# Round two of a graph attention and state-space kernel: one accumulator pair, the D term on TensorE, a scan for the polynomial

## The reference

```python
# layer 1: graph attention on LN(x)
e   = leaky_relu(x @ a[:F] + (x @ a[F:]).T, 0.2)
U   = softmax(where(adj > 0, e, -9e15), axis=1)
prop_u = U @ x;  rowsum = sum(U * 0.5 * U, axis=1)
feat   = soft_threshold(mix of x, prop_u, x * rowsum)
pu     = U @ feat
out    = mix of feat, pu, h0 with coefficients sigmoid(temp)
# layer 2: one Mamba-2 block on LN(x + out), chunks of 128 rows
z, xBC, dt = split(x @ W_in)
xBC = silu(causal conv of 4 taps);  dt = softplus(dt + dt_bias)
Y   = Y_diag + Y_off + xh * D
Y   = Y * silu(z);  Y = Y * rsqrt(mean(Y*Y) + eps) * norm_w
out = (Y @ W_out) @ W_lin + b_lin
```

## Time and profile before

| | |
|---|---|
| three timed runs | 965.16, 971.51, 972.10 us |
| the profiled execution | 977.07 us, span 975.1 us, mean granted TensorE clock 0.935 |
| PE busy | 871.6 us (89%), 6586 matmuls |
| PE weight loads busy | 776.6 us (80%) |
| DVE busy | 771.0 us (79%), 2057 instructions |
| POOL busy | 645.5 us (66%), 1359 instructions |
| ACT busy | 595.4 us (61%), 1032 instructions |
| chain that ended last | POOL 44%, PE 21%, issue 15%, DVE 10%, DMA 5%, ACT 5% |

### The profile page before, as it was taken

One profiled execution on the slowest core, in us unless ns is written; L12 is line 12 of the kernel. 1 busy time (PEld: TensorE's weight loads), 2 busy tenths in 40 slices (PEclk: granted clock), 3 DMA queues, 4 the chain that ended last, 5 costly groups with the idle time before them and its releaser, 6 DMA issues.

```text
span 975.1 us, 21990 instructions
## 1 busy us (share of the span) xinstructions
PE 871.6 (89%) x6586; PEld 776.6 (80%) x6586; DVE 771.0 (79%) x2057; ACT 595.4 (61%) x1032; POOL 645.5 (66%) x1359
## 2 busy tenths in 40 slices
PE   5858999989989999559899898999899989999976
PEld 5648999989989999549788787878778877888844
DVE  6477999979979996576989778777787778688873
ACT  3556788868778885336566556555556656565541
POOL 3550665656665667886768787877776877777743
PEclk9969999999989999859999999999989999899975
DMA  7356887968778686001111111111111111110000
GB/s 212 101 179 216 259 267 215 315 219 267 261 217 279 190 271 203 1 23 61 55 36 56 44 47 47 42 36 48 37 56 32 51 38 51 35 33 17 4 7 9
DMA packets 97386, 110.66 MB, mean 113 GB/s; under 512 B 6433, under 2 KB 89121, under 8 KB 97313
## 3 DMA queue, kind: packets, MB, share of 16 engines
q1 hardware_dynamic: 97312, 109.68, 35.6%
HBM read 90.79 MB, written 18.87 MB: 112 GB/s over the span
## 4 chain that ended last, share of the span: by engine, by line
POOL 44%; PE 21%; issue 15%; DVE 10%; DMA 5%; ACT 5%; POOLq 1%; DVEq 0%; ACTq 0%; SPq 0%
PE accA L1239 6%; POOL featw L510 5%; PE accC L1248 5%; DMA adj_in<-in_adj_dram 4%; POOL f_rows L547 3%; POOL adj_in L545 3%; PE ps L1186 3%; ACT edges L989 3%; POOL adj_in L549 2%; POOL featw L508 2%; POOL ywork L551 2%; POOL f_rows L558 2%; DVE code L642 2%; POOL adj_in L514 1%; POOL featw L513 1%
## 5 line engine op out<-in xcount | busy, mean ns | idle before, releaser
L1239 PE MATMUL accA<-Y,maskA 128*128 128x260 f32 (+1 forms) x2048 | 321.3, 301 | 28.6 <-DVE Y L621 18.1
L1239 PEld LDWEIGHTS accA<-Y,maskA 128*128 128x128 f32 x2048 | 273.7, 198 | 48.5 <-issue 24.6
L1025 ACT ACTIVATE maskA<-code 128x1024 fp32r<-128x1024 int8 x256 | 268.6, 1051 | 58.2 <-PE accC L1248 30.1
L1248 PE MATMUL accC<-Y,maskC 128*128 128x260 f32 (+1 forms) x2048 | 299.3, 290 | 1.4 <-DVE maskC L650 1.4
L1248 PEld LDWEIGHTS accC<-Y,maskC 128*128 128x128 f32 x2048 | 272.6, 196 | 1.9 <-DVE maskC L650 1.8
L650 DVE TENSOR_SCALAR maskC<-code 128x1024 fp32r<-128x1024 int8 x256 | 209.1, 821 | 0.3 <-issue 0.3
L642 DVE SCALAR_TENSOR_TENSOR code<-f_rows,neg_f,ps 128x512 int8<-128x512 f32 x256 | 178.4, 740 | 29.2 <-PE ps L1186 27.8
L989 ACT ACTIVATE edges<-adj_in 128x1024 bf16<-128x1024 f32 x128 | 133.3, 1045 | 27.5 <-DMA adj_in<-in_adj_dram 14.9
L1186 PE MATMUL ps<-ident,edges 128*128 128x128 bf16 x1024 | 82.7, 225 | 16.3 <-DVE code L642 10.8
L870 DVE SCALAR_TENSOR_TENSOR code<-adj_in,f_rows,code 128x128 f32<-128x128 f32 x288 | 94.9, 351 | 0.0
L1186 PEld LDWEIGHTS ps<-ident,edges 128*128 128x128 bf16 x1024 | 60.7, 101 | 27.1 <-issue 12.3
(11 more groups left out here) (199 smaller groups left out, 1588.5 us busy)
## 6 DMA issues: line engine op xcount, KB each, us to landing
adj_in<-in_adj_dram SPq DMA_DIRECT2D x128, 512.0 KB, 4.5
edge_codes<-code SPq DMA_DIRECT2D x8, 2048.0 KB, 10.0
code<-edge_codes SPq DMA_DIRECT2D x32, 512.0 KB, 3.3
xn<-in_x_dram SPq DMA_DIRECT2D x4, 512.0 KB, 5.6
adj_in<-in_x_dram SPq DMA_DIRECT2D x32, 64.0 KB, 1.8
adj_in<-in_L_gnn_h_dram SPq DMA_DIRECT2D x32, 64.0 KB, 1.9
out_dram<-adj_in SPq DMA_DIRECT2D x32, 64.0 KB, 1.6
f_rows<-in_L_ffn_W_in_dram SPq DMA_DIRECT2D x1, 192.0 KB, 6.5
```

The costliest lines, as they stand in the source:

```text
L1025: s.activation(maskA[:, b % MASKS], src, ACT.Relu, bias=-2.0).then_inc(S["maskA_ready"], 1)
L1239: t_.matmul(accA[k][:, 0:2 * cols], maskA[:, b % MASKS, l * P:(l + 1) * P], Y[:, jt, 0, :, 0:cols], start=jt == 0, stop=jt == NT - 1)
L1248: m = t_.matmul(accC[k][:, 0:2 * cols], maskC[:, b % MASKS, l * P:(l + 1) * P], Y[:, jt, 1, :, 0:cols], start=jt == 0, stop=jt == NT - 1)
```

## The change

- **Accumulators.** Round two uses accA0 and accC0 for all row tiles. PE's first product of a slot waits until ACT has read accA (`acc_read`) and DVE has read accC (a new semaphore `c_read`) for the row tile before. ACT's read waits for a new semaphore `a_done`, raised by the last A product, which comes before the last C block; before it waited for both.
- **Banks.** accA1 takes the new state (columns 0 to 255) and the transpose of xn2 (256 to 383); accC1 takes the output product. Before they were in ps1 and ps0. The output product now waits for `out_done`, the state product no longer.
- **C without the turn.** DVE writes C straight from the conv into `cT` (partitions 0 to 63 of a zeroed 128-row tile, two buffers); the product with the identity (L1380) and ACT's copy (L1159) are gone, and the products with C run over 128 rows.
- **D term.** `xD` on POOL (L549) and its addition on DVE (L905) are gone; PE adds the conv output times diag(D) into the chunk product's bank, two products of 128 by 128 by 128 a slot. diag(D) is made once on DVE.
- **Polynomial.** Seven small DVE steps (the square, a scale, four Horner steps, the last product) become one square written five times, one `tensor_tensor_scan` over 24 elements, and one product.
- **Base scalars.** Six POOL operations over all 32 row tiles, once, take the place of a copy and six small operations in each slot.
- **Order.** DVE's output row moves from the head of the slot to behind the gated output. POOL's x1b moves from behind the inverse root to behind the decayed state.
- **Start.** `row_shift` leaves DVE; ACT does it with two Relu activations, and DVE makes two biases. ACT's first two high parts move in between its f1 copies.

```diff
+    def over_rows(i, j):
+        return coef[:, i:j].broadcast_to([P, NT])
+    r_all, zn_all, rho_all, kap_all = (row_out[:, :, i] for i in range(4))
+    link(g.tensor_tensor(kap_all, rho_all, over_rows(1, 2), ALU.mult))
+    link(g.tensor_tensor(kap_all, kap_all, over_rows(8, 9), ALU.add))
+    link(g.tensor_tensor(rho_all, kap_all, over_rows(10, 11), ALU.mult))
+    link(g.tensor_tensor(rho_all, rho_all, over_rows(1, 2), ALU.add))
+    link(g.tensor_tensor(r_all, r_all, rho_all, ALU.mult))
+    link(g.tensor_tensor(zn_all, r_all, zn_all, ALU.mult))
+    end_chain()
...
+    g.memset(state[:], 0.0)
+    g.memset(cT, 0.0)
+    g.memset(horner[:, 0], 0.0)
+    for i in range(6):
+        g.memset(horner[:, 1, :, i], log_c[5 - i])
     g.memset(hist[:, 0, :, 0:TAPS - 1], 0.0).then_inc(S["halo_done"], 1)
...
         wait(pool, f"rowx_in{k % 2}", (s_ - k % 2) * 16 + 32)
-        link(g.tensor_copy(small[:, 8:12], row_out[:, bass.ds(row, 1), :].rearrange("p a b -> p (a b)")))
-        r, zn, rho = (small[:, i:i + 1] for i in (8, 9, 10))
-        link(g.tensor_tensor(kap, coef[:, 1:2], rho, ALU.mult))
-        link(g.tensor_tensor(kap, kap, coef[:, 8:9], ALU.add))
-        link(g.tensor_tensor(wz, kap, coef[:, 10:11], ALU.mult))
-        link(g.tensor_tensor(wz, wz, coef[:, 1:2], ALU.add))
-        wait(pool, "x1_done", s_ - 1)
-        link(g.tensor_tensor(w, wz, r, ALU.mult))
-        link(g.tensor_tensor(wz, w, zn, ALU.mult))
-        link(g.tensor_tensor(featw[:, 0], xn[:, bass.ds(row, 1), :].rearrange("p a b -> p (a b)"),
-                             kap.broadcast_to([P, F]), ALU.mult))
+        step_to(g.tensor_tensor(featw[:, 0], xn[:, bass.ds(row, 1), :].rearrange("p a b -> p (a b)"), kap.broadcast_to([P, F]), ALU.mult))
         link(g.tensor_tensor(featw[:, 1], h0_in[:, k % 2], coef[:, 9:10].broadcast_to([P, F]), ALU.mult))
         link(g.tensor_tensor(featw[:, 0], featw[:, 0], featw[:, 1], ALU.add))
         link(g.tensor_tensor(featw[:, 0], featw[:, 0], x_in[:, k % 2], ALU.add))
+        wait(pool, "x1_done", s_ - 1)
...
-            wait(pool, "y_read", s_ - 3)
-            g.tensor_tensor(heads(xD, HD), heads(xl[:, 0:DI], HD), d_row.unsqueeze(2).broadcast_to([P, NH, HD]), ALU.mult).then_inc(S["xD_ready"], 1)
...
+        if ok[0]:
+            kt = (k - 1) % SLOTS
+            wait(pool, "x1_done", s_)
+            wait(pool, "out_done", s_ - 4)
+            g.tensor_tensor(x1b[:, kt], x1[:, kt % 2], b_row, ALU.add).then_inc(S["x1b_done"], 1)
...
-    def row_shift():
-        step(v.tensor_scalar(hcol[:, 0], fcol[:, :, 0], grow[:, 6:7], 1.0 - SLOPE, ALU.add, ALU.mult))
-        link(v.tensor_scalar(hcol[:, 1], fcol[:, :, 0], grow[:, 6:7], SLOPE - 1.0, ALU.add, ALU.mult))
-        v.tensor_scalar(hcol[:, 0], hcol[:, 0], 0.0, -SHIFT, ALU.min, ALU.add)
-        v.tensor_scalar(hcol[:, 1], hcol[:, 1], 0.0, None, ALU.min).then_inc(S["roww_done"], 1)
...
     v.tensor_scalar(conv_bt, conv_bt, 0.5, None, ALU.mult).then_inc(S["w_ready"], 1)
+    dve.wait_ge(S["signed"], NG * BLOCKS)
+    for kb in range(KB):
...
-            halves = step(v.scalar_tensor_tensor(
-                out=part, in0=accC[kt][:, 0:2 * F].rearrange("p (a b) -> p a b", a=2),
-                scalar=roww[:, bass.ds(row, 1), 1:2].rearrange("p a b -> p (a b)"), in1=acc_s[:, kt, :, 0:F], op0=ALU.mult, op1=ALU.add))
+            dve.wait_ge(S["mm_done"], T * NB + (R1 + NB))
+            v.scalar_tensor_tensor(
+                out=part, in0=accC[0][:, 0:2 * F].rearrange("p (a b) -> p a b", a=2),
+                scalar=roww[:, bass.ds(row, 1), 1:2].rearrange("p a b -> p (a b)"), in1=acc_s[:, kt, :, 0:F],
+                op0=ALU.mult, op1=ALU.add).then_inc(S["c_read"], 1)
...
-        if ok[4]:
-            dve.wait_ge(S["rs_ready"], s_ - 4)
-            wait(dve, f"stored{1 - k2}", (s_ - 5 - (1 - k2)) * 8)
-            v.scalar_tensor_tensor(out=outb[:, 1 - k2], in0=ps[1][:, P:P + F], scalar=tiny[:, 6, 2:3], in1=x1b[:, (k - 1) % SLOTS],
-                                   op0=ALU.mult, op1=ALU.add).then_inc(S["out_done"], 1)
         if ok[0]:
-            dve.wait_ge(S["vch"], halves)
+            dve.wait_ge(S["c_read"], T + 1)
             halves = step(v.tensor_tensor(part[:, 0], part[:, 0], part[:, 1], ALU.add))
...
-                dve.wait_ge(S["xD_ready"], s_ - 3)
                 dve.wait_ge(S["ps_ready"], s_ - 3)
                 summed_y[0] = step(v.tensor_tensor(heads(ysum), heads(ps[0][:, DI:2 * DI]),
                                                    tiny[:, 4 + k2, 0:NH].unsqueeze(2).broadcast_to([P, NH, HD]), ALU.mult))
-                v.tensor_tensor(state[0:DS, 1 - k2], pstate[0:DS], ps[1][0:DS, 0:DI], ALU.add).then_inc(S["st_done"], 1)
-        def y_skip():
-            if ok[3]:
-                dve.wait_ge(S["vch"], summed_y[0])
-                summed_y[0] = step(v.tensor_tensor(ysum, ysum, xD, ALU.add))
+                v.tensor_tensor(state[0:DS, 1 - k2], pstate[0:DS], accA[1][0:DS, 0:DI], ALU.add).then_inc(S["st_done"], 1)
...
-            last = step(v.tensor_tensor(z, si, si, ALU.mult))
+            last = step(v.tensor_tensor(horner[:, 0, :, 1:6], si.unsqueeze(2).broadcast_to([P, NH, 5]),
+                                        si.unsqueeze(2).broadcast_to([P, NH, 5]), ALU.mult))
             conv_step(7)
             dve.wait_ge(S["vch"], last)
-            last = step(v.tensor_scalar(p, z, log_c[-1], None, ALU.mult))
+            last = step(v.tensor_tensor_scan(horner[:, 2].rearrange("p h c -> p (h c)"), horner[:, 0].rearrange("p h c -> p (h c)"),
+                                             horner[:, 1].rearrange("p h c -> p (h c)"), 0.0, ALU.mult, ALU.add))
             conv_step(8)
-            others = [None, None, normalise2, y_state, y_skip]
-            for cf, other in zip(log_c[-2:0:-1] + [None], others):
-                dve.wait_ge(S["vch"], last)
-                if cf is None:
-                    last = step(v.scalar_tensor_tensor(out=p, in0=p, scalar=log_c[0], in1=si, op0=ALU.add, op1=ALU.mult))
-                else:
-                    last = step(v.scalar_tensor_tensor(out=p, in0=p, scalar=cf, in1=z, op0=ALU.add, op1=ALU.mult))
-                if other is not None:
-                    other()
+            dve.wait_ge(S["vch"], last)
+            last = step(v.tensor_tensor(p, horner[:, 2, :, 5], si, ALU.mult))
+            normalise2()
+            y_state()
...
             dve.wait_ge(S["y_read"], s_ - 3)
             wait(dve, "p_yT", s_ - 4)
             wait(dve, "ssq_ready", s_ - 4)
             v.tensor_tensor(yg, ysum, gate[:, k2], ALU.mult).then_inc(S["yg_ready"], 1)
+        if ok[4]:
+            dve.wait_ge(S["p_o"], s_ - 4)
+            dve.wait_ge(S["rs_ready"], s_ - 4)
+            wait(dve, f"stored{1 - k2}", (s_ - 5 - (1 - k2)) * 8)
+            v.scalar_tensor_tensor(out=outb[:, 1 - k2], in0=accC[1][:, 0:F], scalar=tiny[:, 6, 2:3], in1=x1b[:, (k - 1) % SLOTS],
...
-            v.scalar_tensor_tensor(out=xbc[:, k2], in0=gate_t, scalar=1.0, in1=conv, op0=ALU.add, op1=ALU.mult).then_inc(S["conv_ready"], 1)
+            wait(dve, "p_y", s_ - 3)
+            v.scalar_tensor_tensor(out=xbc[:, k2], in0=gate_t, scalar=1.0, in1=conv, op0=ALU.add, op1=ALU.mult)
+            v.scalar_tensor_tensor(out=cT[0:DS, k2], in0=gate_t[DS:P, CB - 1], scalar=1.0, in1=conv[DS:P, CB - 1], op0=ALU.add,
+                                   op1=ALU.mult).then_inc(S["conv_ready"], 1)
...
-        act.wait_ge(S["mm_done"], T * NB + (NB + round_two * R1))
         if round_two:
+            act.wait_ge(S["a_done"], T + 1)
             wait(act, "x1_done", T - 1)
         else:
+            act.wait_ge(S["mm_done"], T * NB + NB)
             wait(act, "scaled_done", T - 1)
         w = roww[:, bass.ds(row, 1), 0:1].rearrange("p a b -> p (a b)")
-        src = accA[k][:, 0:2 * cols].rearrange("p (a b) -> p a b", a=2)
+        src = accA[0 if round_two else k][:, 0:2 * cols].rearrange("p (a b) -> p a b", a=2)
         s.mul(acc_s[:, k, :, 0:cols], src, w).then_inc(S["acc_read"], 1)
...
+            y_high_one(q, 0)
             sign(0, 4)
             f1_copy(3)
+            y_high_one(q, 1)
             f1_copy(4)
             sign(0, 5)
             for c in range(5, 8):
                 f1_copy(c)
-        y_high(q)
+        else:
+            y_high_one(q, 0)
+            y_high_one(q, 1)
+        if q == 0:
+            s.activation(hcol[:, 0], fcol[:, :, 0], ACT.Relu, bias=grow[:, 8:9], scale=SLOPE - 1.0)
+            s.activation(hcol[:, 1], fcol[:, :, 0], ACT.Relu, bias=grow[:, 9:10], scale=1.0 - SLOPE).then_inc(S["roww_done"], 1)
...
+            m = t_.matmul(accA[k][:, 0:2 * cols], maskA[:, b % MASKS, l * P:(l + 1) * P], Y[:, jt, 0, :, 0:cols],
+                          start=jt == 0, stop=jt == NT - 1)
+        if cols == F and ch == NB - 1:
+            m.then_inc(S["a_done"], 1)
...
-                    wait(pe, "x1_done", s_ - 1)
+                    if isinstance(s_, int) and s_ == 0:
```

(38 more changed lines are left out.)

96 lines of the change are left out of this document (46 added, 50 removed).

## The result

The changed kernel takes 997.95 us (median of four, 996.08 to 999.41); the kernel before took 968.92 in the same comparison (four, 965.16 to 972.10). The ratio is 1.030, 95% interval 1.025 to 1.034: slower by 3%. Forecast were 949 us and a range of 929 to 967, and slower by over 1% had a chance of 0.09. The profiled execution took 998.5 us, with a span of 996.8. One execution of a kernel further down, e1_two_pairs, fell in a slow state (1143.8 us, granted clock 0.66) and is left out of its ratio.

The account below looks back on a forecast made before the run. Round two was taken as bound by a POOL-DVE ring. Loop -16, unrolled slots +1.5, diag(D) +0.6, start -5.5 and tail -3 sum to -22.4 us: profiled 977.1 becomes 954.7, median 971.5 becomes 949; range 929 to 967.

Parts of the forecast that it names:

- The new wait: Round two: PE starts block 0 only when both accumulators are read, ACT's read being late; 0.85 us every slot.
- DVE's ring: Round two: chain from DVE's accC read through block 0 and DVE's stream to the next read; 15.6 us a slot.
- The scan's price: DVE's polynomial in round two: the scan taken as 0.17 us, between 0.15 and 0.41.
- The collision rival: Round two: DVE and POOL stretch one another's instructions, slot 16.3 us, 965 us in all; chance 0.24.
- PE's own time: Round two: PE's work without stalls, 14.67 - 0.43 + 0.55 = 14.8 us a slot.
- The clock rival: Round two: the pause at block 0 lowers PE's clock every slot, losing 2 us; slot 17.7, 1001 us; chance 0.09.
- The hidden drain: Round two: ACT reads accA in time, PE alone bounds at 14.8 us a slot; 926 us; chance 0.12.
- First slots: Round two's first slots, 440 to 478 us: some waits won, the drain paid instead; 0.
- POOL's leaving the path: Round two: POOL's chain falls from 13.2 to 11.0 us a slot and no longer bounds it.
- the start: Kernel start: row_shift leaves DVE, whose codes come earlier; -5.5 us, bounds 0 and -7.
- the row's move: Round two: DVE's output row no longer ahead of x1, so POOL's late end no longer starts the next slot; unsized.
- POOL's ring: Round two before the change: POOL's 13.2 us chain plus DVE's 2.3 make the slot, 16.50 us in the loop.

Follow-up runs that it names:

- e1_two_pairs: The changed kernel with two accumulator pairs in round two again, small products' new banks undone too; 898.8 us, ratio 0.924 to the kernel before.
- h1a: The changed kernel with one added wait: POOL's base products start only after DVE's last conv step; 945.7 us, ratio 0.980 to the kernel before.
- g12: e1_two_pairs with DVE's output row back at the slot's head and the base scalars again made slot by slot on POOL; 928.5 us, ratio 0.952.
- h1b: e1_two_pairs with POOL's base products waiting for DVE's last conv step; 892.8 us, ratio 0.926 to the kernel before.
- g6: e1_two_pairs with the zero-padded products taken over 64 rows or 64 columns of weights again; 923.5 us, ratio 0.945 to the kernel before.
- e2: The changed kernel, still one accumulator pair, with DVE reading accC ahead of C's small product and the fourth mask; 937.2 us, ratio 0.965.
- e5: The changed kernel with ten unused transposes on PE at the end of each slot from 4 to 31; 981.3 us, ratio 1.009.
- e4: The kernel before with only the single accumulator pair edits, small products' banks unchanged; 987.8 us, ratio 1.017 to the kernel before.
- g1: e1_two_pairs with DVE's output row back at the slot's head, behind the first mask; 901.2 us, ratio 0.924 to the kernel before.
- g3: e1_two_pairs with the polynomial in seven small DVE steps again; 921.5 us, ratio 0.945 to the kernel before.

## Why the prediction was wrong

**The step that failed is "The new wait", with DVE's ring behind it.** The forecast put the wait at 0.85 us and on ACT, which would be busy up to its read of accA. ACT had read 2.1 us early; DVE held PE for 2.50 us. The forecast had the ring that does this, and sized it at 15.6 us; at the high clock it measures 16.38. By its own pieces: to `in_read` 5.16 (forecast 5.3); L864 to the end of the output row 6.12 (5.4); from there to gm, with C's product, 4.29 (4.05); gm and the read 0.80 (0.8). So 0.7 of the missing 0.8 us is in the stretch that holds the polynomial. The scan's price, 0.17 as a step, was well chosen for a scan alone: it lasts 0.20 in h1a and g12. What was left out is that the base scalars, once removed from POOL, bring POOL's 128-wide products under these very steps, which stretches four of them by 0.93 us in all: the first of these products starts 1.5 us behind L864, where it was 4.0 behind L860 before. There it stood beside two small steps nearer the end (L949 and L952, 0.38 and 0.30 us on the mean), so a part of the stretching is not new. h1a shows the cause, for with the products later that stretch of DVE's stream takes 5.24 us and not 6.12. The collision rival had this mechanism on the masks alone, and gave 16.3 us a slot, the ring's true size. The Trainium skill (SBUF — State Buffer, "Who interferes with whom") says that a DVE instruction with two SBUF inputs contends with a GpSimd instruction that reads SBUF; the trace agrees, 0.43 against 0.17 us for the square.

**PE's own time** was 1.2 too high: 14.8 forecast, 13.61 with nothing in its way (h1b; 13.76 in e1_two_pairs). The padding, costed at nothing, is 0.73 of that by g6 against e1, or 0.88 against h1b. The D products cost 0.45 us by the timeline (0.55 forecast). Between a PE time that was too long and a ring through DVE that was too short the forecast saw two level rings; in truth they are 2.6 us or more apart, and PE pauses for the difference. The ring isn't DVE's load: DVE does the same work in 13.76 us with two pairs (e1). It is a chain through PE, ACT and DVE that only the single pair closes.

**The clock rival** happened in half of the slots. The forecast had it decide from a slot of 16.9 us with 2.5 us at 1.2 GHz in each; measured are 1.37 us in every second one, 0.69 on the mean, so that 16.38 becomes 17.07. Its place was right and its chance, 0.09, too low, for it was hung on a pause of 0.85 that was never measured. That its 1001 us lies beside the measured 998 is luck: it had 2 us of low clock in each slot and the ring at 15.7, where the ring is longer, the clock's share smaller, and the first slots lose 19 us that it had at nothing. Pauses of 1.27 (e2), 1.40 (h1a) and 1.43 us (e5) left the clock up in the loop, and 2.50 did so only in every second slot. The length alone doesn't decide: in e4 the clock fell behind 1.37 us and not behind 1.61. The Trainium skill (TensorE: Matmul & The Clock Gate, "A second HAM failure mode: psum-queue depth-cycling") tells of an oscillation from idle times between groups of matmuls; the trace agrees here, with 0.58 at the head of one slot (700 to 704 us) and 1.00 at the head of the next (716 to 720).

**The hidden drain** (926 us) did not come; the second pair is worth 99 us. The Trainium skill (TensorE: Matmul & The Clock Gate, "HAM oscillation — how this bites in real kernels") reports a kernel in which double buffering in PSUM gained nothing; in this one the measurement says the opposite, and it decides.

**First slots**, forecast at about nothing, were the largest single loss against the kernel before: +16.0 us, and +3.1 in slot 0. Against the forecast the loop is larger, by 27 us, of which the ring and the clock are half each. It is the same wait, since both are gone with two pairs: slot 0 takes 29.1 and slots 1 to 7 88.4 us in e1. POOL's memsets and the whole-row scalars therefore cost nothing that shows. Slots 28 to 30 follow the loop.

**Right were** POOL's leaving the path, the start and diag(D). But the row's move, called the more important part, showed no effect of its own once POOL was short (g1), and the scalars were worth 27 us with the row at the head; the rest of that argument was not run. The start: the first read of accA came at 86.6 us, in the kernel before at 92.0, about the -5.5 that was forecast. Some of it is chance: in e4, which has the old start, it came at 88.7 with the first codes 2.1 us earlier too, so the edit is worth 4 to 5 us. What is left of it at slot 0 can't be read from one profile: kernels that are the same up to there reached slot 0 at 400.9 (e2) to 408.2 us (h1b), and e4 with the old start at 403.9. In the changed kernel DVE makes codes from 47.73 on and the two Relu stand on ACT at 0.33 and 0.31 us, the first of them here:

```profile
45.26 0.33 ACT L1075 ACTIVATE hcol<-fcol,grow 128x32 f32<-128x32 f32 x1
...
47.73 5.36 DVE L668 SCALAR_TENSOR_TENSOR code<-f_rows,neg_f,ps 128x512 int8<-128x512 f32 x8 [0.61 <-PE ps L1193]
```

Diag(D) took 0.27 us for each of its two on DVE. One reading of rows 7 was too strong: L728's 0.17 us was not without POOL, whose next product began 0.01 us behind it, at 54.25; it only came first. The tail gained 7.7 us from slot 31 on and not 3; which of its parts did that was not taken apart, and it varies (57.8 us in e1, 61.7 in h1b, which differ by one wait on POOL).

## What to carry to other kernels

Before giving up a second buffer, follow the release of the one that is left to its place in the reader's stream: what matters is what stands ahead of the read in order, not how long the read is. Such a release can close a chain through several engines that was open before, and the chain can be longer than the work of any one of them: here 16.38 us, with PE and DVE both under 13.8. So its price on the kernel before (1.7%, with POOL's ring still there) says little of its price once that ring is gone (11%). And where work is taken off an engine, ask what moves up into its place, and beside what.

## What the runs showed of the hardware

- A DVE operation on four elements took 0.15 to 0.17 us beside small POOL operations (g12) and 0.34 to 0.42 beside POOL products of 128 by 128 (the changed kernel and g3); the scan over 24 elements took 0.20 (g12, h1a) and 0.46 (the changed kernel), in either place little more than one such step.
- Three groups of fp32 products on 64 rows or with 64 columns of weights, among ones of 128, cost PE 0.73 us a slot over the same ones padded with zeros, some 23 us in 31 slots (g6 against e1_two_pairs).
- Ten unused transposes a slot made the changed kernel 2% faster, by leaving a pause of 1.43 us in place of 2.50 (e5).
- A pause of 2.50 us in every slot of 16.4 brought the granted clock down in every second slot only, and in e4 it fell behind a pause of 1.37 us and stayed up behind one of 1.61.
